# Gate and up weights split partly inside the feed-forward stage, and the projection's normalisation on another engine

## What is computed

```python
h = _layernorm(x, axis=-1) * (1 + ca) + sa
x = x + ga * _L0_attn_ref(h, ...)                     # ends in: ... @ Wo + bo
h = _layernorm(x, axis=-1) * (1 + cb) + sb
x = x + gb * _L0_ffn_ref(h, w_gate, w_up, w_down)

def _L0_ffn_ref(x, w_gate, w_up, w_down):             # 512 -> 2048 -> 512
    gate = jnp.einsum('bsd,hd->bsh', x, w_gate)
    up = jnp.einsum('bsd,hd->bsh', x, w_up)
    gated = jax.nn.silu(gate) * up
    return jnp.einsum('bsh,dh->bsd', gated, w_down)
```

## Time and profile before

| | us |
|---|---|
| median of 3 runs | 2336.63 |
| lowest and highest run | 2335.0 and 2336.87 |
| the profiled execution | 2335.2 |
| its span from the first to the last instruction | 2333.5 |
| TensorE busy in it | 2167.5 (93%) |
| VectorE, ScalarE, GpSimd busy | 1190.7, 788.2, 758.3 |

### The profile page before, as it was taken

The page is one execution under the profiler, slowest core; times in us unless marked ns, Lnnn a source line. Parts: engine busy times, 40 slices in busy tenths (PEclk is TensorE's granted clock), DMA queues, the critical chain, the costliest instruction groups (busy, mean ns, idle before and its releaser), DMA issues. The chain is left out here.

```text
span 2333.5 us, 36753 instructions
## 1 busy us (share of the span) xinstructions
PE 2167.5 (93%) x14056; PEld 1684.2 (72%) x14056; DVE 1190.7 (51%) x2747; ACT 788.2 (34%) x1575; POOL 758.3 (32%) x668
## 2 busy tenths in 40 slices
PE   6989995599999999998687999999999999999998
PEld 3777773377777777775465888888888888888887
DVE  5999996667667667663697122222211222222212
ACT  3333331066665666565355111111111111111111
POOL 2667776121222222222771222222222222222221
PEclk8999997599999999999898999999999999999999
DMA  6132322647575756641896112121111212121111
GB/s 235 58 105 90 108 94 102 154 108 167 127 164 127 165 139 152 152 103 39 261 308 216 54 55 68 50 68 36 60 64 50 68 55 68 50 73 50 53 33 54
DMA packets 164851, 243.99 MB, mean 105 GB/s; under 512 B 20604, under 2 KB 87292, under 8 KB 164184
## 3 DMA queue, kind: packets, MB, share of 16 engines
q1 hardware_dynamic: 160504, 229.27, 34.2%
q0 software_dynamic: 3136, 9.46, 1.3%
q10 hardware_dynamic: 1056, 3.15, 0.3%
HBM read 131.69 MB, written 59.26 MB: 82 GB/s over the span
## 5 line engine op out<-in xcount | busy, mean ns | idle before, releaser
L1363 DVE TENSOR_TENSOR f_gu<-f_psU,f_silu 128x512 f32<-128x512 f32 x128 | 88.5, 692 | 712.3 <-PE f_psU L1430 712.3
L999 ACT ACTIVATE b_probT<-b_psB 128x512 f32<-128x512 f32 (+1 forms) x640 | 316.8, 554 | 170.8 <-PE b_psB L863 168.5
L932 DVE TENSOR_REDUCE b_top<-b_psA 128x2 f32<-128x1024 f32 (+2 forms) x320 | 284.7, 902 | 153.8 <-PE b_psA L840 153.7
L1319 POOL TENSOR_SCALAR f_wd_hi<-f_wd 128x512 fp32r<-128x512 f32 x128 | 83.6, 653 | 823.8 <-PE f_psD L1415 776.2
L1339 ACT ACTIVATE f_silu<-f_psG 128x512 f32<-128x512 f32 x128 | 76.6, 598 | 504.4 <-PE f_psG L1430 504.4
L863 PEld LDWEIGHTS b_psB<-b_stack 98*128 98x128 f32 x1280 | 183.6, 190 | 73.1 <-issue 51.6
L863 PE MATMUL b_psB<-b_stack 98*128 98x256 f32 (+1 forms) x1280 | 218.3, 291 | 6.1 <-ACT b_probT L999 3.9
L1428 PE MATMUL f_psG<-f_hT_hi,w_hi 128*128 128x512 f32 x512 | 200.4, 391 | 11.4 <-DVE f_hT_lo L1357 11.4
L840 PE MATMUL b_psA<-b_stack 96*128 96x512 f32 (+3 forms) x768 | 184.7, 370 | 23.2 <-DMA b_stack<-b_halves 18.0
L1334 ACT ACTIVATE f_gu_hi<-f_gu 128x512 fp32r<-128x512 f32 x128 | 80.9, 632 | 364.5 <-DVE f_gu L1363 364.5
L1429 PE MATMUL f_psG<-f_hT_hi,w_lo 128*128 128x512 f32 x512 | 200.1, 391 | 0.0
(11 more groups left out here) (172 smaller groups left out, 4010.4 us busy)
## 6 DMA issues: line engine op xcount, KB each, us to landing
b_stack<-b_halves SPq DMA_DIRECT2D x192, 256.0 KB, 4.8
f_wd<-in_wd_t SPq DMA_DIRECT2D x128, 256.0 KB, 2.6
qkv_d<-a_t SPq DMA_DIRECT2D x32, 512.0 KB, 2.7
b_land<-qkv_d SPq DMA_DIRECT2D x32, 512.0 KB, 4.2
a_x<-in_x SPq DMA_DIRECT2D x32, 256.0 KB, 3.3
qkv_d<-a_v SPq DMA_DIRECT2D x32, 256.0 KB, 3.1
b_v<-qkv_d SPq DMA_DIRECT2D x16, 512.0 KB, 6.3
att_d<-b_acc SPq DMA_DIRECT2D x16, 512.0 KB, 3.2
```

Of the source, the lines that this page charges most:

```text
L932: last = dve.tensor_reduce(into, tile[:, :, col:col + whole_blocks * P], AX.X, ALU.max, negate=True)
L999: act.activation(probT[:, (NW * n + w) % PROBS, j, 0:width], psB[:, i % BANKS, 0:width], ACT.Exp).then_inc(s["expd"], 1)
```

## The change

**Weights.** In `project_stage` GpSimd now loads and splits only the first four of the sixteen hidden blocks (`EARLY = 4`). A block is 128 hidden columns of both matrices for all four row groups, so 128x1024 elements; it comes in two DMAs of 256 KB each, whose contiguous runs are 512 bytes, and there is one landing buffer. The other twelve blocks are loaded in `ffn_stage` by SP (`load_w`), into the first half of `f_scaled`, which is free until the first token block is done, and split by GpSimd (`split_w`). In units 0 to 11, each engine does block u + 4 before the down weights of unit u. TensorE waits for a block's low part ahead of its gate matrix, and VectorE waits for the last before it first writes f_scaled.

**Normalisation.** VectorE's `norm` now makes the reciprocal and, in a one-column instruction, minus mean times reciprocal (`p_nm`); ScalarE's new step `normal` computes p_xh by one activation (Identity with scale and bias) behind `modulate`. VectorE's `residual` gets a wait for the p_xh of four tiles before, since ScalarE now reads x1.

**Waits.** ScalarE's wait for the modulation columns moves ahead of its first `modulate`, VectorE's for the gate rows ahead of its first `residual`.

```diff
--- before.py
+++ after.py
...
 MASKED = -1e30
 GROUPS = H // 4
 THETA = 30000.0
+EARLY = 4
 def at_least(eng, sem, value):
...
-    PIECE = HID // 4
...
         mv = sb("p_mv", [P, 4, 2])
         sd = sb("p_sd", [P, 4])
         rs = sb("p_rs", [P, 4])
+        nm = sb("p_nm", [P, 4])
         h2 = sb("p_h2", [P, 4, KC, P])
         spots = sb("p_spots", [1, 4])
-        wland = sb("p_wland", [P, 2, PIECE])
+        wland = sb("p_wland", [P, 2, KC, P])
         psP = ctx.enter_context(nc.psum_tensor("p_psP", [P, 2, DM], F32))
         psT = ctx.enter_context(nc.psum_tensor("p_psT", [P, 2, DM], F32))
 
...
         x_in = [sem(f"p_x_in{j}") for j in range(4)]
         x1_out = [sem(f"p_x1_out{j}") for j in range(4)]
         h2_out = [sem(f"p_h2_out{j}") for j in range(4)]
-        piece_in = [sem(f"p_piece_in{j}") for j in range(2)]
+        piece_in = sem("p_piece_in")
         block = ctx.enter_context(nc.Block())
 
         def done(b, t):
             return b * TB + (t + 1)
+
+        def twice(b, t, n):
+            return b * (2 * TB) + (2 * t + n)
 
         def uses(b, t):
 
...
                     with nc.allow_non_contiguous_dma(reason="a few columns"):
                         pool.dma_start(mod2[:, n, b], scratch["mod"][b, 3 + n, :].rearrange("(k p) -> p k", p=P)).then_inc(s["mod_in"], 16)
 
-            PIECES = [(k, m, h) for k in range(KC) for m in range(2) for h in range(4)]
-
-            def load_piece(n):
-                k, m, h = PIECES[n]
-                at_least(pool, s["piece_lo"], n - 1)
-                src = args["wu_t" if m else "wg_t"][k * P:(k + 1) * P, h * PIECE:(h + 1) * PIECE]
-                pool.dma_start(wland[:, n % 2], src).then_inc(piece_in[n % 2], 16)
-
-            load_piece(0)
-            for n, (k, m, h) in enumerate(PIECES):
-                if n + 1 < len(PIECES):
-                    load_piece(n + 1)
-                cols = slice(h * PIECE, (h + 1) * PIECE)
-                pool.wait_ge(piece_in[n % 2], 16 * (n // 2 + 1))
-                pool.tensor_scalar(w_hi[:, m, k, cols], wland[:, n % 2], 1.0, 1.0, ALU.mult, ALU.mult).then_inc(s["piece_hi"], 1)
-                pool.wait_ge(s["piece_hi"], n + 1)
-                pool.tensor_tensor(w_lo[:, m, k, cols], wland[:, n % 2], w_hi[:, m, k, cols].bitcast(F32), ALU.subtract).then_inc(s["piece_lo"], 1)
+            for c in range(EARLY):
+                cols = slice(c * P, (c + 1) * P)
+                at_least(pool, s["piece_lo"], c)
+                for m, name in enumerate(("wg_t", "wu_t")):
+                    pool.dma_start(wland[:, m], args[name].rearrange("(k p) n -> p k n", p=P)[:, :, cols]).then_inc(piece_in, 16)
+                pool.wait_ge(piece_in, 32 * c + 32)
+                pool.tensor_scalar(w_hi[:, :, :, cols], wland[:], 1.0, 1.0, ALU.mult, ALU.mult).then_inc(s["piece_hi"], 1)
+                pool.wait_ge(s["piece_hi"], c + 1)
+                pool.tensor_tensor(w_lo[:, :, :, cols], wland[:], w_hi[:, :, :, cols].bitcast(F32), ALU.subtract).then_inc(s["piece_lo"], 1)
 
         @block.scalar
         def _(act):
...
                 act.wait_ge(s["mv"], done(b, t))
                 act.activation(sd[:, t % 4:t % 4 + 1], mv[:, t % 4, 1:2], ACT.Sqrt, bias=eps[:, 0:1]).then_inc(s["sd"], 1)
 
+            def normal(b, t):
+                act.wait_ge(s["rs"], twice(b, t, 2))
+                at_least(act, s["turned"], done(b, t - 2))
+                act.activation(xh[:, t % 2], x1[:, t % 4], ACT.Identity, scale=rs[:, t % 4:t % 4 + 1],
+                               bias=nm[:, t % 4:t % 4 + 1]).then_inc(s["xh"], 1)
+
             def modulate(b, t):
-
+                if isinstance(b, int) and b == 0 and t == 0:
+                    act.wait_ge(s["mod_in"], 16 * 2 * B)
                 at_least(act, h2_out[t % 4], uses(b, t - 4))
                 pause(nc, act, spots[:, t % 2:t % 2 + 1], psT[0:1, t % 2, 0:1], s["turned"], done(b, t))
                 for k in range(KC):
...
                     last = act.activation(h2[:, t % 4, k], psT[:, t % 2, k * P:(k + 1) * P], ACT.Identity, bias=m[0], scale=m[1])
                 last.then_inc(s["h2_ready"], 1)
 
-            act.wait_ge(s["mod_in"], 16 * 2 * B)
-            stagger(act, B, TB, [(root, 3), (high, 0), (modulate, 4)])
+            stagger(act, B, TB, [(root, 3), (high, 0), (modulate, 4), (normal, 3)])
 
         @block.vector
         def _(dve):
...
                 dve.tensor_tensor(at_lo[:, t % 2], at[:, t % 4], at_hi[:, t % 2].bitcast(F32), ALU.subtract).then_inc(s["at_lo"], 1)
 
             def residual(b, t):
+                if isinstance(b, int) and b == 0 and t == 0:
+                    dve.wait_ge(s["gate_in"], 16 * B)
                 dve.wait_ge(s["projected"], done(b, t))
                 g = gate[:].rearrange("p b n -> p (b n)")[:, bass.ds(b * DM, DM)]
                 dve.tensor_tensor(gated[:, t % 2], psP[:, t % 2], g, ALU.mult).then_inc(s["gated"], 1)
                 dve.wait_ge(x_in[t % 4], uses(b, t))
                 at_least(dve, x1_out[t % 4], uses(b, t - 4))
+                at_least(dve, s["xh"], done(b, t - 4))
                 dve.wait_ge(s["gated"], done(b, t))
                 dve.tensor_tensor(x1[:, t % 4], gated[:, t % 2], x[:, t % 4], ALU.add).then_inc(s["x1"], 1)
                 dve.wait_ge(s["x1"], done(b, t))
...
             def norm(b, t):
                 dve.wait_ge(s["sd"], done(b, t))
                 dve.reciprocal(rs[:, t % 4:t % 4 + 1], sd[:, t % 4:t % 4 + 1]).then_inc(s["rs"], 1)
-                at_least(dve, s["turned"], done(b, t - 2))
-                dve.wait_ge(s["rs"], done(b, t))
-                dve.tensor_scalar(xh[:, t % 2], x1[:, t % 4], mv[:, t % 4, 0:1], rs[:, t % 4:t % 4 + 1],
-                                  ALU.subtract, ALU.mult).then_inc(s["xh"], 1)
-
-            dve.wait_ge(s["gate_in"], 16 * B)
+                dve.wait_ge(s["rs"], twice(b, t, 1))
+                dve.scalar_tensor_tensor(out=nm[:, t % 4:t % 4 + 1], in0=mv[:, t % 4, 0:1], scalar=-1.0, in1=rs[:, t % 4:t % 4 + 1],
+                                         op0=ALU.mult, op1=ALU.mult).then_inc(s["rs"], 1)
+
             stagger(dve, B, TB, [(norm, 3), (residual, 2), (low, 0)])
 
         @block.tensor
...
         psD = ctx.enter_context(nc.psum_tensor("f_psD", [P, 4, DM], F32))
 
         x1 = land[:].rearrange("p t k q -> p t (k q)")
-
-        names = ("h_in h_hi h_lo gate_mm up_mm silu gu gu_hi gu_lo wd_hi wd_lo down down_t "
+        wland = scaled[:, 0:2].rearrange("p m (k q) -> p m k q", q=P)
+
+        names = ("h_in h_hi h_lo gate_mm up_mm silu gu gu_hi gu_lo split_hi wd_lo w_in w_lo down down_t "
                  "scaled final").split()
         s = {n: sem("f_" + n) for n in names}
         wd_in = [sem(f"f_wd_in{j}") for j in range(2)]
...
                     sp.wait_ge(s["final"], 4 * i + t + 1)
                     sp.dma_start(out[i * 4 + t:i * 4 + t + 1].rearrange("a p n -> p (a n)"), x1[:, t]).then_inc(out_done, 16)
 
+            def load_w(c):
+                at_least(sp, s["w_lo"], c - EARLY)
+                for m, name in enumerate(("wg_t", "wu_t")):
+                    src = args[name].rearrange("(k p) n -> p k n", p=P)[:, :, c * P:(c + 1) * P]
+                    sp.dma_start(wland[:, m], src).then_inc(s["w_in"], 16)
+
             load_h(0)
             for u in range(NU + 3):
                 i, c = u // HC, u % HC
+                if u + EARLY < HC:
+                    load_w(u + EARLY)
                 if u < NU:
                     load_wd(u)
                 if c == 2 and 1 <= i <= NB:
...
 
         @block.gpsimd
         def _(pool):
+            def split_w(c):
+                cols = slice(c * P, (c + 1) * P)
+                pool.wait_ge(s["w_in"], 32 * (c - EARLY + 1))
+                pool.tensor_scalar(w_hi[:, :, :, cols], wland[:], 1.0, 1.0, ALU.mult, ALU.mult).then_inc(s["split_hi"], 1)
+                pool.wait_ge(s["split_hi"], 2 * (c - EARLY) + 1)
+                pool.tensor_tensor(w_lo[:, :, :, cols], wland[:], w_hi[:, :, :, cols].bitcast(F32), ALU.subtract).then_inc(s["w_lo"], 1)
+
             for u in range(NU):
+                if u + EARLY < HC:
+                    split_w(u + EARLY)
                 at_least(pool, s["down"], u - 1)
                 pool.wait_ge(wd_in[u % 2], 16 * (u // 2 + 1))
-                pool.tensor_scalar(wd_hi[:, u % 2], wd[:, u % 2], 1.0, 1.0, ALU.mult, ALU.mult).then_inc(s["wd_hi"], 1)
-                pool.wait_ge(s["wd_hi"], u + 1)
+                pool.tensor_scalar(wd_hi[:, u % 2], wd[:, u % 2], 1.0, 1.0, ALU.mult, ALU.mult).then_inc(s["split_hi"], 1)
+                pool.wait_ge(s["split_hi"], u + 1 + min(u + 1, HC - EARLY))
                 pool.tensor_tensor(wd_lo[:, u % 2], wd[:, u % 2], wd_hi[:, u % 2].bitcast(F32), ALU.subtract).then_inc(s["wd_lo"], 1)
 
         @block.scalar
...
 
             def scale(i, t):
                 if t == 0:
+                    dve.wait_ge(s["w_lo"], HC - EARLY)
```

(2 more changed lines are left out.)

## The result

| | before | after |
|---|---|---|
| median, us | 2336.75 (4 runs) | 2315.43 (4 runs) |
| lowest and highest run | 2335.0 and 2337.93 | 2315.28 and 2315.89 |
| ratio of the medians, 95% interval | | 0.9909 [0.9895, 0.9923] |
| span of the profiled execution | 2333.5 | 2313.6 |

What follows compares the result with a forecast made beforehand. VectorE, slowed beside GpSimd's splitting, bounds the projection loop, TensorE the feed-forward part. -6.0 - 19.7 + 2.0 + 1.0 + 1.3 + 1.0 = -20.4 us, from 2335.2 to 2314.8, plus 1.4 for the median: 2316.2 us; range 2311 to 2331.

Steps and rivals of the forecast that it cites:

- Start, -6.0: Start of the projection: with the wait for modulation columns moved, the first at_lo begins 5.98 us earlier; -6.0 us.
- TensorE's 3.71 is then the floor: Projection loop over 32 tiles: TensorE then sets 3.71 us a tile, 116.3 in place of 136.0; -19.7 us.
- Splitting, +2.0: Projection loop: the four blocks still split there by GpSimd slow VectorE at the earlier ratio; +2.0 us, at most 13.8.
- Loop turns, +1.0: Projection loop, body run three times: jumps so far hidden behind VectorE may show; +1.0 us, between 0 and 3.1.
- Tail, +1.3: End of the projection: the last tile's normal stands behind modulate of the tile before; +1.3 us, between 0 and 2.4.
- Feed-forward start, +1.0: Start of the feed-forward stage: one of VectorE's four subtracts may wait for a wider GpSimd split; +1.0 us, 0 to 3.5.
- Ring: First feed-forward block: issue, landing and split of weights through one buffer take 7.65 us a block, at cost 0.
- the threshold: First feed-forward block: up to 8.8 us a block costs nothing; past it TensorE waits 11 us for each further microsecond.
- Rival 1: First feed-forward block: weights land too slowly, 12.3 us a block, TensorE waits 38.5 us, total 2354.7 us; chance 0.08.
- Rival 2: Projection loop and feed-forward start: long GpSimd splits hold VectorE for their full length, total 2330.5 us; chance 0.09.
- Rival 3: Projection loop: ScalarE's normal or late landings keep the period at about 4.0 us, 8.7 more, total 2324.9 us; chance 0.13.
- A: Projection loop, theory made after the result: VectorE set the 3.71, so moving the normalisation gives 0.24 us a tile more.

Runs made afterwards that it cites:

- the longer ring: The changed kernel with the subtract done twice in each of the twelve blocks split in the feed-forward part; 2327.83 us, ratio 0.9962.
- one block early: The changed kernel with one of sixteen blocks split in the projection stage and fifteen in the feed-forward part (EARLY = 1); 2308.21 us, ratio 0.9873.
- two blocks early: The changed kernel with two blocks split in the projection stage and fourteen in the first feed-forward block (EARLY = 2); 2311.14 us, ratio 0.9897.
- one load for four blocks: The changed kernel with only the first block of weights loaded in the projection and split four times, into blocks 0 to 3; 2313.94 us, ratio 0.9908.

## Why the prediction was right, and where it was not

- **Start, -6.0.** Right: -5.8 in the change, -6.0 with the waits alone. VectorE's splitting of Wo is what is late next: it ends at 1119.87 and the first at_lo begins at 1119.91. But a loop that starts earlier meets tiles of att that are not there yet, and with the waits alone 4.1 us reach the median.
- **"TensorE's 3.71 is then the floor": wrong.** It gave 30 x 3.71; the period came out at 3.47, 0.24 x 30 = 7.2 us less. The step that failed is the reading of the earlier trace rows, that the transposes end where the bias matmul begins, "so TensorE sets the pace there". That end is modelled. VectorE's share of 18.33 in 20.00 us was the sign against it, and at_lo's end 0.05 us ahead of each bias matmul would have shown it.
- **Splitting, +2.0: undersized; it is +8.0 together with the late tiles of att.** "I take the ratio" failed in four ways. The normalisation's 0.33 a tile was taken out as gone, but with the normalisation only VectorE is held for as long as before (20.8 and 21.0 us). The 86.8 us of GpSimd that it was divided by hold some 17 us in which GpSimd issues loads; its splitting was 69.6, while the 13.8 that it was multiplied with are splitting alone. The ratio was carried over from splits of 0.6 to 1.3 us to splits of 2.4 to 2.7, and the held share of a microsecond of splitting went from 0.30 to 0.62. And the new one-column instruction, which I had priced by its columns, has 4.6 of the 9.1 us held. For the old width the run with the normalisation only gives the ratio itself: 127.80 - 1.72 - 31 x 3.47 = 18.5 us of loop beside 69.6 of splitting, which would be 3.9 for 14.7 us, late tiles of att included. The transfers had no term at all: 4.2 us are left where nothing is held, and ScalarE's wait for att is 7.8 and 12.2 us in two runs of the same stage, 6.9 with the waits alone, and 0.3 before.
- The two errors, -7.2 and +6.0, nearly cancel. That is luck; the total, 0.9 us off by the change of the medians, was closer than its terms deserve.
- **Loop turns, +1.0.** Nothing: from the 12th interval on all are 3.46 to 3.49, the loop's later turns among them. The 1.02 us of idle time in the earlier trace rows, which ended with VectorE's at_lo, is no cost of the turn as such.
- **Tail, +1.3.** 1.9 in the profiled run, 1.5 in most others (11.9). Its cause was right: with normal ahead of modulate it is 10.2, as with the normalisation on VectorE (10.1 to 10.4).
- **Feed-forward start, +1.0.** 0.4 (one of VectorE's four subtracts took 2.85 us and TensorE waited 0.61). **Ring:** 7.65 forecast and 7.65 measured, cost 0; the longer ring fits the threshold.
- **Rivals.** Rival 1 didn't come. Rival 2 had the right mechanism, with instructions that lasted 2.2 and 2.3 us where 2.5 was named; it priced the loop at 13.8 and the feed-forward start at 3.5, and 8.0 (late att included) and 0.4 came, which A's gain covered. Rival 3 has its sign too: transposes waited for p_xh, 2.6 us between 1119 and 1165, but not in the steady loop.

## What to carry to other kernels

Before you call an engine the floor, take the distance between its instructions' starts and look for another engine's instruction that ends right before each round begins; modelled busy time hides waits of 0.2 us a tile. Price a new instruction on VectorE beside a GpSimd instruction that reads SBUF by what may hold it, and not by its size: one column with two SBUF inputs took up to 2.17 us for 0.16. Wider splits held more per microsecond here. Taking a held instruction off the engine need not take the held time off, if another one is as exposed. When a wait at the start of a pipeline goes, ask whether the loads can follow that much earlier. And before you read a wait's change as an effect, see how far it moves where nothing was changed.

## What the runs showed that I had not expected

TensorE's clock at the beginning of the feed-forward part comes back at different times. The view by stretches of five microseconds, first of the changed kernel, then of the one with one block early (TensorE's granted clock is the third number from the end; 0.50 is the level of 1.2 GHz):

```profile
1259.00:1264.00 5.00, 4.21 (x9) 2.81 (x9) 4.96 (x4) 2.85 (x5) 3.73 (x3) 0.50 0.18 57
1264.00:1269.00 5.00, 4.39 (x19) 3.67 (x20) 1.22 (x2) 0.60 (x1) 3.57 (x5) 0.97 0.50 157
```

```profile
1254.00:1259.00 5.00, 4.07 (x9) 2.84 (x9) 4.82 (x4) 2.99 (x5) 3.60 (x2) 0.50 0.24 72
1259.00:1264.00 5.00, 4.39 (x11) 3.39 (x11) 0.69 (x1) 0.60 (x1) 3.49 (x4) 0.50 0.52 157
```

Both have the same matrices to multiply and the same 0.61 us of idle time, which ends 4.8 us after the first matmul (that is at 1259.79 in the one, at 1254.93 in the other). In the second the clock stays low for some five microseconds more; the first gate to first up matmul takes 6.26 us in place of 5.62, and the rest 1049.51 in place of 1048.19: 2.0 us in all. The weights alone, two blocks early and one load for four blocks have it too (6.28, 6.29 and 6.28 us). The cause is open. It is 2.0 us of a profiled execution that the change in a kernel need not have made.
